# The first score pass of a 16-head attention, two heads at a time on the two 64-row halves of the TensorE array

## The chip, the cores and the metric

The kernel runs on one core of one Trainium2 chip. The metric is the device time of the whole program in microseconds; the median of several runs counts. The kernel is one program for all sixteen batch rows of a two-layer block, with everything written out ahead of time: each engine has one straight list of instructions, and the order in each list comes from timetables in the source.

## The reference, cut to what matters

The block has an attention and a feed-forward part in layer 0 (16 heads of 8 dimensions over 512 tokens, then eight experts of which each token uses one), and a windowed attention and a two-layer local transformer in layer 1. The change concerns the layer 0 attention alone:

```python
x_h = x.reshape(b, t, h, d).transpose(0, 2, 1, 3)      # 16 heads, d = 8, t = 512
xw  = jnp.einsum('bhtd,hde->bhte', x_h, w_att_val)
att = jnp.einsum('bhte,bhse->bhts', xw, x_h) / jnp.sqrt(d)
att = jax.nn.softmax(att, axis=-1)                     # then att @ values, projection
```

So each batch row needs, for each of 16 heads, a 512x512 matrix of scores, its row maxima, its exponentials and their product with the values.

## The kernel before

The scores are wanted at nearly float32 precision from bf16 products. Queries and keys are therefore split into three bf16 parts (`SPLIT = 3`), and all nine products of a part with a part are summed in one contraction: a "stack" of 3 x 3 x 8 = 72 rows (`STACK`) holds for each head the matching parts of the queries (`Qst_a`) and of the keys (`Kst_a`). The scores are computed twice. The first pass (L1436, and L1424 for group 0) contracts 72 rows with queries on the output partitions; VectorE takes the maximum of each 128x512 result (L1583, L1571). The maxima, in two bf16 parts, are turned by TensorE (`turned_parts`, L677), copied by ScalarE (L1518, L1535) and put by one DMA (`max_to_stack`, L1359) into rows 72 and 73 of `Qst_a`, beside rows of ones in `Kst_a`. The second pass (L1466) contracts these 74 rows with keys on the output partitions, so that the maxima come off in the product, and ScalarE takes the exponential (L1523). The products with the values are L1452, eight records for each key tile, on column strips of 32.

The heads are worked in four groups of four. A group has 16 first-pass and 16 second-pass products (4 heads x 4 tiles). The stacks lie in a ring of two. While group g is in its second pass, group g+1 is in its first pass: in `a_tensor` the two alternate, product by product. Group 0's first pass lies apart, in `head_tensor`, in the stage before.

The stacks are filled through DRAM. SyncE's queue issues 8 DMAs that spill the parts (`spill`, L1343 and L1345), and then for each group 6 DMAs that load the stack (`load_stack`, L1354 and L1355; each of 24 rows by 4 heads by 1 KB). Groups 0 and 1 are loaded once the spill is there, group 2 when the last second-pass product of group 0 is made, group 3 when the last of group 1 is made (`a_sync`). In SyncE's list the DMA for the maxima of group 1 stands behind the load of group 2, and that of group 2 behind the load of group 3. SyncE runs its list strictly in order.

Around this, in one stage of the loop (`rows`), five streams are woven: this attention for one batch row, the layer 1 windowed attention (`b`) and the `head` of following rows, and the local transformer (`f`, `feed`) of the rows before. `TIMES` gives each stream's slots a place, `merge` sorts them on each engine, and the result is the fixed order. The score products share six PSUM banks (`SEATS` gives each product its bank, `Banks.take` waits until the product before it in that bank has been read). The opening, which does row 0 among the gating and expert work, uses three banks in turn and its own tables (`OPEN`).

In TensorE's order of before, one stage counts 95 places where the next instruction uses another division of the array (full array, column strips of 32 or 64, row parts of 32 or 64, or both). Between the last second-pass product of group 1 and the first of group 3's first pass lie one transposition of 4, two L2023 groups of 16, L1452 x8, L677 x4, L2033 x8 and five transpositions of 4.

Of the kernel before, what the change touches and what calls it, by code (L numbers as in the profile page):

```python
# [23 lines left out]
P = 128  # L24
# [227 lines left out]
                  (-147.32851, -146.32851)),  # L252
            "head": ((0, 9.5, 12, 17, 29.6),
                  (-161.91197, -159.15848, -159.15847, -128.18067, -121.88243)),
            "f": ((0, 8.1, 14.2),
                  (-262.83466, -259.50354, -168.69272)),
            "a": ((34, 36, 56, 59, 83),
                  (-262.9151, -260.55741, -246.75033, -239.1571, -236.47977)),
            "finish": ((14.7, 15.7),
                  (-227.09831, -226.09831))},  # L260
        "gpsimd": {
            "gate": ((0, 1),
                  (-80.93999, -79.93999)),
            "b": ((0.5, 1.5),
                  (-35.02612, -34.02612)),
            "head": ((1, 2),
                  (5.75878, 6.75878)),
            "f": ((5, 6.5, 10.4, 11.9, 15.8, 17.3, 21.2, 22.7, 47, 70, 71.5, 75.4, 76.9, 80.8, 82.3, 86.2, 87.7),
                  (-152.95046, -106.77442, -105.48318, -102.87694, -87.68456, -81.66902, -67.27071, -43.44755, -39.3071, -23.9864, -17.3062, 7.99167, 10.6375, 17.73295,
                   17.73296, 17.73297, 19.90829)),  # L270
            "feed": ((6.8, 7.8),
                  (-153.62176, -152.62176))},
# [6 lines left out]
            "head": ((4.5, 6, 16, 16.7, 17.4, 18.1, 18.8, 19.5, 20.2, 20.9, 21.6, 22.3, 23, 23.7, 24.4, 25.1, 25.8, 26.5, 29),  # L279
# [108 lines left out]
    "b": "015310413113055204155111345013352422",  # L388
    "head": "05202254021041231030",
    "f": ("415401435215345124031214215041450140224254013451510305204325341205231045204354324130414230"  # L390
          "4532032410025041"),
    "feed": "033035420"}
B_AT = 5
LAYER = 65
# [2052 lines left out]
```

## Time and profile before

| | |
|---|---|
| median of 3 runs | 3223.6 us (3221.94 to 3223.61) |
| profiled execution | 3225.27 us, span 3223.5 us |
| TensorE busy | 2973.0 us, 92% of the span |
| VectorE, ScalarE busy | 2333.2 and 2309.6 us, 72% each |
| granted TensorE clock, mean | 0.964 |

The opening takes the first 366 us; after that the stages repeat, each some 176 us long. Busy shares say where time is occupied, not what ends a wait; the matmul records are pipelined and their ends are modelled, so for TensorE the distance from start to start is the price of an instruction, and a busy TensorE still has small gaps.

### The profile page before, as it was taken

To read this page: it belongs to the slowest core of one execution; us is meant where nothing else is said; L and a number is where in the kernel's file an instruction comes from. 1 tells how busy PE (TensorE), PEld (TensorE's weight loads), DVE (VectorE), ACT (ScalarE), POOL (GpSimd) and SP (SyncE) were. 2 spreads that over 40 slices of the span, in tenths; PEclk is the share of its full clock that TensorE was granted. 3 is DMA by queue.
4 is the path that set the end of the run, shared out by engine and by line. 5 is a ranking of instruction groups with operands and counts; after the bars stand their busy time and mean duration, and the time that the engine had idled before them with its cause. 6 is when DMAs were issued, how large, how long until landed. Compare 5 with 4: busy or idle time off the path is not lost.

```text
span 3223.5 us, 84708 instructions
## 1 busy us (share of the span) xinstructions
PE 2973.0 (92%) x34588; PEld 1863.0 (58%) x34588; DVE 2333.2 (72%) x4989; ACT 2309.6 (72%) x4768; POOL 1221.3 (38%) x778
## 2 busy tenths in 40 slices
PE   5799699999999999999999999999999999999976
PEld 5269446556565656565565656565555656565654
DVE  6732487878686878878786868788787868687744
ACT  4453277787777787877777777868777777778754
POOL 1124044433333443444433334334444333344344
PEclk9689799999999999999999999999999999999988
DMA  4437200101011111011010101111110101111000
GB/s 135 118 117 208 60 23 24 42 15 44 25 33 36 34 32 37 25 33 33 15 46 23 41 28 34 33 36 32 32 29 15 46 23 34 35 33 33 6 14 4
DMA packets 128575, 134.10 MB, mean 42 GB/s; under 512 B 18100, under 2 KB 111070, under 8 KB 128190
## 3 DMA queue, kind: packets, MB, share of 16 engines
q1 hardware_dynamic: 123648, 119.37, 13.5%
q0 software_dynamic: 4544, 9.32, 1.3%
q8 instruction: 278, 4.55, 0.6%
q14 instruction: 105, 0.86, 0.1%
HBM read 81.06 MB, written 30.28 MB: 35 GB/s over the span
## 4 chain that ended last, share of the span: by engine, by line
PE 53%; ACT 21%; DVE 8%; issue 3%; SPq 2%; DMA 2%; POOL 1%; ACTq 0%; POOLq 0%; DVEq 0%
PE bank L1452 6%; PE bank L1466 5%; ACT area L2109 5%; PE bank L2047 5%; PE bank L1436 4%; ACT prob_a L1523 4%; PE bank L2023 3%; PE bank L2091 3%; PE bank L2014 3%; PE bank L671 3%; PE bank L2033 3%; PE bank L1986 2%; PE bank L2004 2%; PE bank L1424 2%; PE bank L1744 2%
## 5 line engine op out<-in xcount | busy, mean ns | idle before, releaser
L1523 ACT ACTIVATE prob_a<-bank 128x512 f32<-128x512 f32 x1024 | 554.0, 606 | 137.0 <-PE bank L1466 134.0
L1583 DVE TENSOR_REDUCE nmax_a<-bank 128x1 f32<-128x512 f32 x768 | 497.8, 683 | 96.5 <-PE bank L1436 93.5
L1953 POOL TENSOR_TENSOR rn<-ss,minus_half 128x16 f32<-128x16 f32 x128 | 391.7, 3060 | 223.1 <-DVE ss L2221 222.8
L1976 POOL TENSOR_TENSOR rs_f<-rs_f,minus_half 128x4 f32<-128x4 f32 x32 | 32.5, 1017 | 1076.5 <-DVE rs_f L1311 1076.5
L1466 PE MATMUL bank<-Qst_a,Kst_a 74*128 74x512 bf16 x1024 | 375.5, 391 | 12.3 <-ACT prob_a L1523 8.6
L2109 ACT ACTIVATE area<-bank 128x512 f32<-128x512 f32 x640 | 350.5, 610 | 49.5 <-PE bank L2047 46.5
L1959 POOL TENSOR_TENSOR turn_f<-turn_f 128x512 f32<-128x512 f32 x256 | 332.1, 1317 | 127.1 <-DVE turn_f L2226 127.1
L2226 DVE TENSOR_TENSOR turn_f<-area,rotf 128x1024 f32<-128x1024 f32 x256 | 305.6, 1216 | 5.8 <-POOL area L1963 5.4
L1436 PE MATMUL bank<-Kst_a,Qst_a 72*128 72x512 bf16 x768 | 302.7, 394 | 5.0 <-DMA Kst_a<-dk_a 2.3
L1452 PE MATMUL bank<-prob_a,V_a 128*18 128x512 f32 x2048 | 278.0, 615 | 16.1 <-ACT prob_a L1523 13.2
L1963 POOL TENSOR_TENSOR area<-turn_f,rn 128x1024 f32<-128x1024 f32 x128 | 243.5, 1902 | 18.3
L2233 DVE TENSOR_REDUCE nmax_f<-bank 128x4 f32<-128x512 f32 x256 | 167.2, 685 | 70.8 <-PE bank L2004 70.7
L1436 PEld LDWEIGHTS bank<-Kst_a,Qst_a 72*128 72x128 bf16 x768 | 75.3, 98 | 219.9 <-ACT prob_a L1523 96.8
L2047 PE MATMUL bank<-wqkv_s,hT_f 128*128 128x512 f32 x384 | 178.8, 603 | 20.5 <-ACT hT_f L2109 20.5
L2047 PE MATMUL bank<-wqkv_s,hT 128*128 128x512 f32 x384 | 195.3, 605 | 0.0
L1466 PEld LDWEIGHTS bank<-Qst_a,Kst_a 74*128 74x128 bf16 x1024 | 96.4, 98 | 164.9 <-ACT prob_a L1523 64.0
L2091 PE MATMUL bank<-xnT_f,w_s 128*128 128x512 f32 (+1 forms) x384 | 183.2, 615 | 2.7 <-ACT xnT_f L2109 2.7
L1986 PE MATMUL bank<-ident,area 128*128 128x128 f32 x1024 | 155.3, 280 | 23.9 <-ACT kq_a L1512 12.9
L1571 DVE TENSOR_REDUCE nmax_a<-bank 128x1 f32<-128x512 f32 x256 | 159.8, 675 | 14.4 <-PE bank L1424 12.8
L1912 DVE TENSOR_REDUCE max_b<-bank 128x8 f32<-128x512 f32 x192 | 130.7, 681 | 53.7 <-PE bank L1734 53.4
L2217 DVE TENSOR_REDUCE ss_tiny<-area 128x16 f32<-128x1024 f32 x128 | 154.1, 1204 | 15.6 <-ACT area L2109 15.6
L1808 ACT ACTIVATE oT_a<-bank 128x512 f32<-128x512 f32 x96 | 58.2, 606 | 132.7 <-PE bank L1744 132.6
(307 smaller groups left out, 6766.0 us busy)
## 6 DMA issues: line engine op xcount, KB each, us to landing
Qst_a<-dq_a SPq DMA_DIRECT2D x192, 96.0 KB
Kst_a<-dk_a SPq DMA_DIRECT2D x192, 96.0 KB
area<-in_W SPq DMA_DIRECT2D x25, 512.0 KB, 4.7
dq_a<-prob_a SPq DMA_DIRECT2D x80, 128.0 KB
V_f<-in_W SPq DMA_DIRECT2D x14, 512.0 KB, 4.9
dk_a<-prob_a SPq DMA_DIRECT2D x48, 128.0 KB
ys_d<-otok_f SPq DMA_DIRECT2D x39, 128.0 KB, 3.8
x_a<-in_x_in SPq DMA_DIRECT2D x16, 256.0 KB, 2.8
```

Source lines behind the costliest of these rows:

```text
L1436: nc.tensor.matmul(bk.take(pe, f)[:], Qst_a[0:STACK, g % RING, j, t * P:(t + 1) * P], Kst_a[0:STACK, g % RING, j, :], start=True, stop=Tru ...
L1452: last = nc.tensor.matmul(acc_a[32 * j:32 * j + 2 * (D0 + 1), :], V_a[:, k, 4 * g + j, :], prob_a[:, (4 * k + j) % PR_A, :], start=(g % 2 ...
L1466: nc.tensor.matmul(bk.take(pe, s)[:], Kst_a[0:ROWS, g % RING, j, k * P:(k + 1) * P], Qst_a[:, g % RING, j, :], start=True, stop=True).then ...
L1523: nc.scalar.activation(dst, bk.full(act, product)[rows, :], func, **kw).then_inc(a_emptied["act"], 1)
L1583: nc.vector.tensor_reduce(out=nmax_a[:, g, t, j:j + 1], in_=bk.full(dve, f)[:], op=ALU.max, axis=AX.X, negate=True).then_inc(emptied, 1)
L1953: nc.gpsimd.tensor_tensor(rn[:, t % 2], ss[:, t % 2], minus_half[:], ALU.pow).then_inc(f_root, 1)
L1959: last = nc.gpsimd.tensor_tensor(cos[:, :, :, lo:lo + 32], cos[:, :, :, lo:lo + 32], sin[:, :, :, hi:hi + 32], ALU.add)
L1963: nc.gpsimd.tensor_tensor(qk_raw[:, t % 2].rearrange("p a (h d) -> p a h d", d=FD), turned[:, :, 0].rearrange("p a (h d) -> p a h d", d=FD ...
L2047: nc.tensor.matmul(fk.take(pe, (product, l, t))[:], (hT if l == 0 else hT_f)[:, t * P:(t + 1) * P], wqkv_s[:, l, n * INNER:(n + 1) * INNER ...
L2091: nc.tensor.matmul(fk.take(pe, (product, l, c))[0:n, :], w1_s[:, l, col:col + n], xnT_f[:], start=True, stop=True).then_inc(f_filled, 1)
L2109: ins = nc.scalar.activation(dst, fk.full(act, product)[rows, cols], func, **kw)
L2226: last = nc.vector.tensor_tensor(turned[:, a].rearrange("p c (h d) -> p c h d", d=FD), raw[:, a].rearrange("p (h d) -> p h d", d=FD).unsqu ...
```

## The change

Heads of a group are taken in pairs, an even and an odd one. Even heads keep their stack in rows 0 to 71 with the maxima in rows 72 and 73. Odd heads have theirs in the upper half: the first 64 stack rows in array rows 64 to 127, the last 8 in rows 0 to 7, the maxima in rows 32 and 33 beside ones, and zeros in the other rows of 0 to 63, written once at the start. The first pass contracts 64 rows only (the product of the last parts is left out of it, and the parts are spilled in another order so that this is the smallest one), the even head on rows 0 to 63 and the odd head on rows 64 to 127, one right after the other into two banks. Both banks are taken before the first of the two is issued. The second pass of odd heads contracts all 128 rows. A group's stack is loaded by 14 DMAs in place of 6 (even and odd heads apart, and the odd heads' last part in two pieces), and its maxima by two DMAs in place of one. The first-pass products of a group stand in the order head 0, head 1 for each query tile, then heads 2 and 3, and a pair has one slot, before two second-pass products.

All tables of `TIMES` and `SEATS` are new; `OPEN` and `STEP` are as before. The numbers in the tables are places in an order, and the streams' order is what they amount to. On TensorE one stage now crosses 136 times between divisions of the array, and 32 pairs stand where 64 products stood. Group 0's eight pairs come after the last windowed scores of stream `b`, where before the first two of its products stood ahead of them. Between the last second-pass product of group 0 and group 2's first pair stand two transpositions of 4 and two L2047 products more than before; between the last of group 1 and group 3's first pair the same pieces as before, in another order (transposition, L2023 x16, L1452 x8, L677 x4, L2023 x16, L2033 x8, five transpositions). SyncE's order around the loads is unchanged: load of group 2, maxima of group 1, load of group 3, maxima of group 2, maxima of group 3.

```diff
@@ TIMES (all streams of all engines are new; one of them) @@
-            "head": ((4.5, 6, 16, 16.7, 17.4, 18.1, 18.8, 19.5, 20.2, 20.9, 21.6, 22.3, 23, 23.7, 24.4, 25.1, 25.8, 26.5, 29),
...
+            "head": ((4.5, 6, 16, 17.4, 18.8, 20.2, 21.6, 23, 24.4, 25.8, 29),
+                  (12.75675, 14.24365, 45.14976, 45.14977, 50.14609, 50.47676, 50.59673, 55.58908, 55.58909, 58.57354, 64.32902)),
...
-        Kst_a, Qst_a = sb("Kst_a", [P, RING, 4, T], BF16), sb("Qst_a", [ROWS, RING, 4, T], BF16)
+        Kst_a, Qst_a = sb("Kst_a", [P, RING, 4, T], BF16), sb("Qst_a", [P, RING, 4, T], BF16)
...
+            for tile in (Kst_a, Qst_a):
+                nc.vector.memset(tile[0:64, :, 1::2, :], 0.0)
...
+            nc.vector.memset(Kst_a[32:34, :, 1::2, :], 1.0)
...
-        first = [[("first", g, j, t) for j in range(4) for t in range(NT)] for g in range(G)]
+        first = [[("first", g, 2 * i + odd, t) for i in range(2) for t in range(NT) for odd in range(2)] for g in range(G)]
...
-                sp.dma_start(dq[:, c], parts_q[:, c % SPLIT, :]).then_inc(s, 16)
+                sp.dma_start(dq[:, c], parts_q[:, (c + 1) % SPLIT, :]).then_inc(s, 16)
...
-        SPILLED, STACKED = (3 * SPLIT - 1) * 16, 2 * SPLIT * 16
-
-        def load_stack(sp, dq, dk, h, n, Qst, Kst, s):
+        SPILLED, STACKED = (3 * SPLIT - 1) * 16, 14 * 16
+
+        def load_stack(sp, dq, dk, h, Qst, Kst, s):
 
             rows = SPLIT * D0
-            q_rows, k_rows = (d[h:h + n].rearrange("h c d t -> (c d) h t") for d in (dq, dk))
-            for i in range(SPLIT):
-                sp.dma_start(Qst[rows * i:rows * i + rows], q_rows[D0 * i:D0 * i + rows]).then_inc(s, 16)
-                sp.dma_start(Kst[rows * i:rows * i + rows], k_rows).then_inc(s, 16)
+            for odd in range(2):
+                q_rows, k_rows = (d[h + odd:h + 4:2].rearrange("h c d t -> (c d) h t") for d in (dq, dk))
+                for i in range(SPLIT):
+                    for lo, hi, at in (((0, 16, 112), (16, 24, 0)) if odd and i == SPLIT - 1 else ((0, rows, 64 * odd + rows * i),)):
+                        sp.dma_start(Qst[at:at + hi - lo, odd::2], q_rows[D0 * i + lo:D0 * i + hi]).then_inc(s, 16)
+                        sp.dma_start(Kst[at:at + hi - lo, odd::2], k_rows[lo:hi]).then_inc(s, 16)
...
-            sp.dma_start(Qst[STACK:ROWS, :, :], mT).then_inc(landed, 16)
+            for odd, at in enumerate((STACK, 32)):
+                sp.dma_start(Qst[at:at + 2, odd::2, :], mT[4 * odd:4 * odd + 4, :]).then_inc(landed, 16)
...
+        def first_pair(r, pe, bk, g, n):
+            if n == 0:
+                pe.wait_ge(*nth(r, a_stack[g], STACKED))
+            pair = [(bk.take(pe, f), f) for f in first[g][n:n + 2]]
+            for ps, (_, _, j, t) in pair:
+                rows = slice(64 * (j % 2), 64 * (j % 2) + 64)
+                nc.tensor.matmul(ps[:], Qst_a[rows, g % RING, j, t * P:(t + 1) * P], Kst_a[rows, g % RING, j, :],
+                                 start=True, stop=True).then_inc(a_filled, 1)
+
...
             for g in range(G):
                 for n in range(16):
-                    yield A_GROUP[g] + 1.2 * n
-                    if g + 1 < G:
-                        first_pass(g + 1, n)
+                    if g + 1 < G and n % 2 == 0:
+                        yield A_GROUP[g] + 1.2 * n
+                        first_pair(r, pe, bk, g + 1, n)
                     yield A_GROUP[g] + 1.2 * n + 0.4
                     if n == 0:
-                        pe.wait_ge(*nth(r, a_mrow[g], 16))
+                        pe.wait_ge(*nth(r, a_mrow[g], 32))
                     _, _, k, j = s = second[g][n]
-                    nc.tensor.matmul(bk.take(pe, s)[:], Kst_a[0:ROWS, g % RING, j, k * P:(k + 1) * P], Qst_a[:, g % RING, j, :],
+                    nc.tensor.matmul(bk.take(pe, s)[:], Kst_a[0:(P if j % 2 else ROWS), g % RING, j, k * P:(k + 1) * P],
+                                     Qst_a[0:(P if j % 2 else ROWS), g % RING, j, :],
                                      start=True, stop=True).then_inc(a_filled, 1)
```

## Rows read from the trace of the kernel before

**Rows 1.** The page: busy time of the engines; granted TensorE clock in 40 slices, in tenths.
```profile
PE 2973.0 (92%) x34588; PEld 1863.0 (58%) x34588; DVE 2333.2 (72%) x4989; ACT 2309.6 (72%) x4768; POOL 1221.3 (38%) x778
...
PEclk9689799999999999999999999999999999999988
```

**Rows 2.** Windows: one stage; length, busy of PE, PEld, DVE, ACT, POOL, clock, DMA.
```profile
1062.04:1238.35 176.32, 167.89 (x2078) 102.58 (x2075) 139.05 (x289) 137.52 (x288) 70.76 (x44) 1.00 0.12 32
```

**Rows 3.** The chain that ended last by engine (page), and one of the waits.
```profile
PE 53%; ACT 21%; DVE 8%; issue 3%; SPq 2%; DMA 2%; POOL 1%; ACTq 0%; POOLq 0%; DVEq 0%
...
ACT prob_a L1523 <- PE bank L1466: 134.0, 194, 2.7
```

**Rows 4.** Groups by line and shape, PE: count, busy us, mean ns, idle before.
```profile
L1466 PE MATMUL bank<-Qst_a,Kst_a 74*128 74x512 bf16 x1024 | 375.5, 391 | 12.3 <-ACT prob_a L1523 8.6 <-DVE nmax_a L1583 2.9 <-DMA Qst_a<-Kst_a 0.5
L1436 PE MATMUL bank<-Kst_a,Qst_a 72*128 72x512 bf16 x768 | 302.7, 394 | 5.0 <-DMA Kst_a<-dk_a 2.3 <-ACT prob_a L1523 2.1 <-DVE nmax_a L1583 0.6
...
L1424 PE MATMUL bank<-Kst_a,Qst_a 72*128 72x512 bf16 x256 | 85.4, 410 | 22.5 <-DMA Kst_a<-dk_a 20.4 <-DVE nmax_a L1571 1.6 <-ACT og_a L1808 0.3
```

**Rows 5.** The chain in order of time, in group 2's first pass: start, length.
```profile
1343.02 0.22 PE bank L1466
1343.24 0.98 PE bank L1452 x8
1344.22 0.32 PE bank L1436
```

**Rows 6.** Timeline of PE where two row parts of the array work together.
```profile
1239.32 1.05 PE L1417 MATMUL bank<-wv_s,kq_a 128*128 128x128 f32 x8
1240.30 0.39 PE L1702 MATMUL bank<-lat_q,lat_of 32*128 32x512 bf16 x2
1240.53 1.02 PE L1707 MATMUL bank<-spare_b,prob_a 32*128 32x256 f32 x8
```

**Rows 7.** Timeline of SyncE's queue: load of group 3 (first and last of 6), maxima of group 2.
```profile
1345.23 0.30 SPq L1354 DMA_DIRECT2D Qst_a<-dq_a  x1
...
1347.24 0.38 SPq L1355 DMA_DIRECT2D Kst_a<-dk_a  x1
1348.73 0.63 SPq L1359 DMA_DIRECT2D Qst_a<-Kst_a  x1
```

**Rows 8.** Windows of 1 us over that load (last columns: DMA share, GB/s).
```profile
1348.23:1349.23 1.00, 1.00 (x11) 1.00 (x11) 0.00 (x0) 0.98 (x2) 0.00 (x0) 1.00 0.82 167
...
1350.23:1351.23 1.00, 1.00 (x12) 0.99 (x11) 0.69 (x4) 0.83 (x3) 0.00 (x0) 1.00 0.00 0
```

**Rows 9.** Timeline of PE: group 1's last second pass, then groups 3 and 2.
```profile
1344.82 0.38 PE L1466 MATMUL bank<-Qst_a,Kst_a 74*128 74x512 bf16 x1
...
1351.18 0.38 PE L1436 MATMUL bank<-Kst_a,Qst_a 72*128 72x512 bf16 x1
1351.40 0.38 PE L1466 MATMUL bank<-Qst_a,Kst_a 74*128 74x512 bf16 x1
```

**Rows 10.** Timeline of the opening: a DMA of maxima and the product that waits.
```profile
98.79 0.77 SPq L1359 DMA_DIRECT2D Qst_a<-Kst_a  x1
...
100.94 0.61 PE L1466 MATMUL bank<-Qst_a,Kst_a 74*128 74x512 bf16 x1 [0.51 <-DMA Qst_a<-Kst_a]
```

**Rows 11.** The chain in order of time: the last DMA of a load of group 0.
```profile
2866.91 4.48 DMA Kst_a<-dk_a
```

**Rows 12.** Timeline of VectorE in group 0's first pass: eight maxima, the split.
```profile
1283.46 4.86 DVE L1571 TENSOR_REDUCE nmax_a<-bank 128x1 f32<-128x512 f32 x8
...
1293.45 0.17 DVE L1335 TENSOR_REDUCE mparts_a<-nmax_a 128x16 bf16<-128x16 f32 x1
```

**Rows 13.** Windows of 5 us: VectorE (fourth figure) before and during group 0's pass.
```profile
1268.00:1273.00 5.00, 4.78 (x159) 3.67 (x158) 3.93 (x10) 4.35 (x13) 0.00 (x0) 1.00 0.51 141
...
1283.00:1288.00 5.00, 5.00 (x82) 3.99 (x84) 4.96 (x11) 2.31 (x4) 0.00 (x0) 1.00 0.02 5
```

**Rows 14.** Timeline of VectorE at the start, behind the memsets.
```profile
13.57 1.64 DVE L1077 BATCH_NORM_STATS2 spare_b<-V_s 128x6 f32<-128x128 f32 x8 [6.31 <-DMA V_s<-in_x_in]
```

More of the change, by code:

```diff
@@ L676, in turned_parts @@
             for t in range(NT):
-                last = nc.tensor.matmul(dst[MT, t * P:(t + 1) * P], parts[:, t].rearrange("p a j -> p (a j)"), ident_bf[:],
+                last = nc.tensor.matmul(dst[MT, t * P:(t + 1) * P], parts[:, t].rearrange("p o a j -> p (o a j)"), ident_bf[:],
                                         start=True, stop=True)
@@ L1265, in mixer_kernel @@
             for n in range(16):
-                if g + 1 < G:
-                    plan_a.append((A_GROUP[g] + 1.2 * n, first[g + 1][n], ["dve"]))
+                if g + 1 < G and n % 2 == 0:
+                    plan_a += [(A_GROUP[g] + 1.2 * n, f, ["dve"]) for f in first[g + 1][n:n + 2]]
                 plan_a.append((A_GROUP[g] + 1.2 * n + 0.4, second[g][n], ["act"]))
@@ L1418, in head_tensor @@
             last.then_inc(a_filled, 1)
-            for n, f in enumerate(first[0]):
-                _, _, j, t = f
+            for n in range(0, 16, 2):
                 yield 16 + 0.7 * n
-                if n == 0:
-                    pe.wait_ge(*nth(r, a_stack[0], STACKED))
-                nc.tensor.matmul(bk.take(pe, f)[:], Qst_a[0:STACK, 0, j, t * P:(t + 1) * P],
-                                 Kst_a[0:STACK, 0, j, :], start=True, stop=True).then_inc(a_filled, 1)
+                first_pair(r, pe, bk, 0, n)
             yield 29
@@ L1430, in a_tensor @@
         def a_tensor(r, pe, bk, hk):
-            def first_pass(g, n):
-                _, _, j, t = f = first[g][n]
-                if n == 0:
-                    pe.wait_ge(*nth(r, a_stack[g], STACKED))
-                nc.tensor.matmul(bk.take(pe, f)[:], Qst_a[0:STACK, g % RING, j, t * P:(t + 1) * P],
-                                 Kst_a[0:STACK, g % RING, j, :], start=True, stop=True).then_inc(a_filled, 1)
             def max_rows(g):
@@ L1570, in head_vector @@
                 yield 16 + 0.7 * n
-                nc.vector.tensor_reduce(out=nmax_a[:, 0, t, j:j + 1], in_=bk.full(dve, f)[:], op=ALU.max, axis=AX.X,
+                nc.vector.tensor_reduce(out=nmax_a[:, 0, t, top_at(j):top_at(j) + 1], in_=bk.full(dve, f)[:], op=ALU.max, axis=AX.X,
                                         negate=True).then_inc(emptied, 1)
@@ L1574, in head_vector @@
             dve.wait_ge(*bk.brought(first[0][-1], "dve"))
-            yield from split_max(28.1, link, nmax_a[:, 0], [mparts_a[:, 0, :, p, :] for p in range(2)], h_mparts)
+            yield from split_max(28.1, link, nmax_a[:, 0], [mparts_a[:, 0, :, :, p, :] for p in range(2)], h_mparts)
         def a_vector(r, dve, bk, link, after_finish=False):
@@ L1582, in first_pass @@
                 _, _, j, t = f = first[g][n]
-                nc.vector.tensor_reduce(out=nmax_a[:, g, t, j:j + 1], in_=bk.full(dve, f)[:], op=ALU.max, axis=AX.X,
+                nc.vector.tensor_reduce(out=nmax_a[:, g, t, top_at(j):top_at(j) + 1], in_=bk.full(dve, f)[:], op=ALU.max, axis=AX.X,
                                         negate=True).then_inc(emptied, 1)
@@ L1587, in max_parts @@
                 dve.wait_ge(*bk.brought(first[g][-1], "dve"))
-                yield from split_max(A_GROUP[g - 1] + 19.6, link, nmax_a[:, g], [mparts_a[:, g, :, p, :] for p in range(2)], a_mparts)
+                yield from split_max(A_GROUP[g - 1] + 19.6, link, nmax_a[:, g], [mparts_a[:, g, :, :, p, :] for p in range(2)], a_mparts)
             for g in range(G):
```

76 lines of the change are left out of this document (39 added, 37 removed), and 125 rows, old and new, of the table TIMES.

## The prediction

> **What bounds the kernel now.** I read the page first: TensorE is busy 92% of the span, VectorE and ScalarE 72% each, and after the opening's slices its granted clock is at full (9 or more tenths) until the end [rows 1]. Then the windows of one stage: of 176.3 us TensorE is busy 167.9, VectorE 139.1, ScalarE 137.5, at a granted clock of 1.00 [rows 2]. Then the chain that ended last: TensorE carries 53% of it, ScalarE 21%, VectorE 8%, and the largest waits between engines are those of ScalarE's exponentials for their scores [rows 3]. So TensorE's issue order sets the pace, with the two others near enough to take over where the order gets denser. The stage repeats from 366 us to about 3000 us, and fifteen batch rows pass through it; the sixteenth lies in the opening. A microsecond per stage is 15 us, or 0.5%.
>
> The groups by line [rows 4] show what is touched: 768 + 256 first-pass products and 1024 second-pass ones. Their means (391 to 410 ns) are latencies; the price is the distance from start to start, 0.22 us each in the chain [rows 5].
>
> **What the pairs save.** Two products on different row parts of the array overlap: the two 32-row products of L1702 start together at 1240.30 and the next instruction starts at 1240.53, so 512 bf16 columns through two row parts cost 0.23 us in place of 0.44 [rows 6]. That is with 32-row parts and not 64, the nearest row there is. 64 products become 32 pairs, 32 x 0.21 = 6.7 us a stage. If the halves did not overlap, nothing of this would be saved; the row speaks against that.
>
> **What they cost TensorE.** Each change of the array's division has a price. In the chain a first-pass product that follows a plain one takes 0.22, one that follows the column strips of L1452 takes 0.32 [rows 5]; going into row parts, eight records of L1417 at 0.11 are 0.88 and the next start is 0.98 behind the first [rows 6]. So about 0.095 a crossing. The old order has 95 crossings a stage and the new one 136, counted in the two timetables: 41 x 0.095 = 3.9 us. A pair inside full-array work pays 0.19 for a gain of 0.21; it is the eight pairs of group 0, which lie partly together, and those that stand beside L1452 or another strip, that earn. Net 6.7 - 3.9 = 2.8 us. The 128-row second pass of odd heads costs nothing: a full-array product of as many columns costs the same whatever the rows in it are (L1436 with 72 rows and L1466 with 74, 0.22 both), and I know no dearer row.
>
> The Trainium skill says the same in TensorEngine Tiling (Array Packing), Key Properties: changing the tiling mode drains the array. It gives no price. With the 0.095 of the row the rule eats more than half of the gain; read as free, the sum would be 15 x 3.9 = 58 us lower.
>
> **What the loads cost.** A load is 14 DMAs on one queue in place of 6. The six of group 3 start 0.40 us apart (five steps from 1345.23 to 1347.24), one takes 0.30 to 0.38 [rows 7]. I take 0.40 for the smaller ones too, since no row shows a DMA's issue getting cheaper with fewer rows; the lower bound is 0.34 (0.30 and 0.04 between), the upper 0.67, the pitch of the DMA for the maxima, which has only eight runs [rows 7]. Landing of the last one: a small one lets its waiter go 2.15 us after it started (98.79 to 100.94) [rows 10]; the last of six takes 4.48 [rows 11], but there six large ones are backed up, and the transfers run at 167 GB/s until they are through [rows 8]. Fourteen halves at one in 0.40 us ask for about 120 GB/s (48 KB each) and don't back up, so I take 2.1. Load to landing: 13 x 0.40 + 2.1 = 7.3 us, where six took between 5 and 6.
>
> *Group 3.* The load starts at 1345.23, when group 1's last second-pass product is through, and group 3's first product stands at 1351.18: 5.95 us [rows 9]. The new order has the same pieces there and two more crossings, 6.15 us. So TensorE waits 7.3 - 6.15 = 1.15 us. Then comes what is queued behind the loads: the maxima of group 2. Before, the queue was free at 1347.6 and their DMA went out at 1348.73 [rows 7]. Now the queue is free 5.6 us after the load's start, the second of two DMAs starts 0.67 later, at 6.3, and lets go at 8.4. The first second-pass product of group 2 would stand 0.32 behind the pair, at 7.6; it waits 0.8 more. Together 2.0 us a stage, all on TensorE, with nothing to cover it since its list is in order. With 0.34 a DMA: 4.4 + 2.1 = 6.5 and 7.6, together 0.9. With 0.67: 10.8 and 12.2, together 5.7.
>
> *The other groups.* Between its release and its first product group 2's load had about 7 us of pieces (the pieces of both orders reckoned at the chain's prices, here and below) and now gets two transpositions and two 0.86 us products more, almost 10: covered. Group 0's pairs stand 4.5 us later in the order, its load lands 1 us later: covered, and the wait that L1424 shows now, 20.4 us over the run of which most in the opening [rows 4], goes where it was in the stages, 0.3 us each. Group 1's load has 15 us to spare. The two DMAs of maxima cost 0.67 more before each second pass; the spaces there grew by 0.2 to 0.8 and had 0.8 to spare: nothing.
>
> **VectorE in group 0's pass.** Eight maxima take 4.86 us, 0.61 each [rows 12]. From TensorE's first pair to L677 the new order needs 11.1 us, the old 16.6. VectorE has 16 x 0.61 = 9.7 in that stretch, 1.2 of other work laid between, and the split, 0.9 with its neighbour: 11.8. It becomes the bound by 0.7, of which 0.2 was already lost there. Before the pass it has room that it can't use (3.93 of 5 us), in the pass none (4.96 of 5) [rows 13]. I count +0.5, from 0 (if it runs ahead) to 3.0 (if other work slides in). The pairs take two banks at once; where VectorE is late by one reduction, TensorE waits for both. With six banks I count this within that range.
>
> **Start and opening.** The memsets lie ahead of a 6.31 us wait of VectorE [rows 14]: nothing. In the opening the three loads with little room cost up to 2 us each and the pairs save some of it at half clock; three banks make pairs stiffer. I take +2, from -5 to +8.
>
> **Sum.** A stage: -2.8 - 0.3 + 2.0 + 0.5 = -0.6 us. Fifteen: -9. With +2 for the opening, -7 on the profiled 3225.27 us, which lies 1.7 above the median: 3218 by the profile, 3216.6 against the median. Predicted: 3217 us.
>
> **Rivals.** (1) *The loads don't hold TensorE.* If small DMAs issue in 0.34 and the wait at group 3 lets ScalarE and VectorE catch up, so that later waits (for `prob_a`, 134 us over the run in ScalarE's favour [rows 3]) shrink by as much: -2.8 to -3.1 a stage, 15 x -2.9 + 2 = -42, 3182 us. For it: at 1350 VectorE has little to do [rows 8] and could bank time; against it: TensorE is busy nearly all of that stretch, and a wait in an in-order list is rarely given back.
>
> (2) *The queue is the bound: slower.* Place: group 3's first pair and group 2's first second-pass product. Price: 5.7 us a stage at 0.67 a DMA. Stage: -3.1 + 5.7 + 0.5 = +3.1; fifteen and +4 in the opening give +50, 3274 us. It decides from 0.44 us a DMA on: there the wait is 2.6 and the stage is no faster. For it: the issue price has not followed size in any row; half way, at 0.53, it is 3245.
>
> (3) *Nothing comes out.* The results must still be read: 16 maxima a group at 0.61 us and 16 exponentials besides. Where a pair and two second-pass products stand close (0.23 + 0.19 + 0.44 = 0.86 us), VectorE needs 1.2. A shorter TensorE then waits at the banks for what it saved; stage within 0.3 of before, 3224 us. The Trainium skill has this as PSUM Bottleneck, in TensorEngine Tiling (Array Packing): tiling speeds TensorE up, not the reading of PSUM. For it: VectorE at 4.96 of 5 [rows 13]; against it: 37 us of slack a stage [rows 2].
>
> **How the numbers follow.** Forecast 0.36, rival 1 0.20, rival 2 0.24, rival 3 0.20. Its own range for the forecast is 3200 to 3232. The range that holds 8 in 10 goes from 3178 (most of rival 1) to 3262 (rival 2 up to a DMA price of about 0.6). About 0.2%, 6.5 us, is what a measurement can tell. Faster by more: 0.21 of the forecast's 0.36, 0.20, 0.02 of rival 3: 0.43. Within: 0.11 and 0.13: 0.24. Slower: 0.04, 0.24 and 0.05: 0.33.
>
> **What would show it.** After: pairs 3 to 5 ns apart with the next start 0.23 or 0.32 us on; stages of 175 to 176 us; an idle of about 1.2 us before group 3's first pair with a stack DMA as its releaser, and about 0.8 before group 2's second pass with the DMA of the maxima; L677 of group 0 waiting for VectorE. The prediction is wrong in its core if the issue pitch of the 14 DMAs isn't near 0.40, if the halves don't overlap, or if the waits at the banks of the score products grow by more than a microsecond a stage.

## The result, and the profile after

The changed kernel takes 3269.35 us (median of 3257.69, 3269.35 and 3271.68) against 3223.6: 1.0134 times before, interval 1.0096 to 1.0172. It is slower, by 46 us, where 3217 was forecast; the time also lies above the range. In a later job, copies of both kernels side by side gave 1.0138 (1.0111 to 1.0164). One caution goes with every ratio below: the kernel before has two levels, 3223 to 3229 us in some jobs and 3281 to 3291 in others, and the changed kernel takes 3268 beside either. Each run names its "before"; what the higher level is comes at the end.

The page after answers to [rows 1, 3]. TensorE's busy time reads 2943 us for 2973, but 172 matmul records of L1469 are missing from this trace; in the copy of the changed kernel, whose records are complete, it is 2967. So TensorE is busy for about as long as before, in a longer span. Its share of the chain fell from 53 to 48%, ScalarE's rose from 21 to 26%. Then the groups of the two passes, which answer to [rows 4].

```profile
PE 2943.1 (90%) x34416; PEld 1821.9 (56%) x34588; DVE 2348.5 (72%) x4992; ACT 2321.1 (71%) x4768; POOL 1243.0 (38%) x778
...
PEclk9699799999999999999999999999999999999988
...
PE 48%; ACT 26%; DVE 6%; issue 4%; SPq 3%; DMA 1%; POOL 1%; POOLq 0%; ACTq 0%; DVEq 0%
...
L1469 PE MATMUL bank<-Qst_a,Kst_a 74*128 74x512 bf16 (+1 forms) x852 | 292.0, 395 | 23.9 <-DMA Qst_a<-Kst_a 8.7
L1455 PE MATMUL bank<-prob_a,V_a 128*18 128x512 f32 x2048 | 277.7, 615 | 26.1 <-ACT prob_a L1527 18.9
L1419 PE MATMUL bank<-Kst_a,Qst_a 64*128 64x512 bf16 x1024 | 203.4, 399 | 54.3 <-DMA Kst_a<-dk_a 19.7
```

One stage of after, as a window (columns as in [rows 2]): as long as a stage of before plus 1.8 us. (Ten PE records are missing from it.)

```profile
1082.49:1260.57 178.08, 166.39 (x2068) 99.92 (x2075) 139.97 (x289) 138.38 (x288) 72.23 (x44) 1.00 0.11 31
```

The place that the prediction names, group 3's load and group 2's maxima, in the timeline of SyncE's queue and of PE (answers to [rows 7, 9]). Fourteen DMAs, 0.41 us apart (one takes 1.17), then the two of the maxima; the first pair 7.7 us after the load's start. This is one of the stages with a slow DMA; most have none, and their first pair stands at 7.17 us (below).

```profile
1544.28 0.30 SPq L1355 DMA_DIRECT2D Qst_a<-dq_a  x1
1544.62 0.37 SPq L1356 DMA_DIRECT2D Kst_a<-dk_a  x1
1545.04 0.37 SPq L1355 DMA_DIRECT2D Qst_a<-dq_a  x1
...
1548.35 1.17 SPq L1355 DMA_DIRECT2D Qst_a<-dq_a  x1
...
1550.39 0.29 SPq L1356 DMA_DIRECT2D Kst_a<-dk_a  x1
1550.72 1.28 SPq L1364 DMA_DIRECT2D Qst_a<-Kst_a  x2
```

```profile
1552.01 0.39 PE L1419 MATMUL bank<-Kst_a,Qst_a 64*128 64x512 bf16 x2 [0.62 <-DMA Kst_a<-dk_a]
1553.16 0.39 PE L1469 MATMUL bank<-Qst_a,Kst_a 74*128 74x512 bf16 x1 [0.76 <-DVE nmax_a L1587]
```

The pairs themselves, in the chain in order of time: both products in the time of one, and 0.32 us to the next start.

```profile
1543.39 0.32 PE bank L1419 x2
1543.71 0.55 PE bank L1469
```

**Where the time went.** I cut each of the 14 inner stages at the starts of four kinds of TensorE instructions: the stage's first product (xw), the turning of a group's maxima (mT0 to mT3) and a group's first second-pass product (s0 to s3). Mean lengths in us; "before" and "changed" are the two copies that ran on one chip (b_copy, a_copy), "order" and "loads" are two experiments that follow:

| stretch | before | changed | order alone | loads alone |
|---|---|---|---|---|
| xw to mT0 (group 0's first pass in it) | 56.84 | 56.61 | 56.60 | 59.37 |
| mT0 to s0 | 4.23 | 4.93 | 4.93 | 4.24 |
| s0 to mT1 (group 1's first pass) | 24.10 | 23.64 | 23.91 | 24.09 |
| mT1 to s1 | 4.69 | 4.83 | 4.85 | 5.77 |
| s1 to mT2 (group 2's first pass) | 20.36 | 20.64 | 20.97 | 20.48 |
| mT2 to s2 (maxima, behind group 3's load) | 3.73 | 5.72 | 4.55 | 6.10 |
| s2 to mT3 (group 3's first pass) | 15.22 | 15.57 | 15.95 | 17.00 |
| mT3 to the next xw | 46.84 | 46.73 | 46.73 | 46.84 |
| stage | 176.01 | 178.67 | 178.49 | 183.90 |
| opening, to the first xw | 363.6 | 370.7 | 370.6 | 372.7 |

TensorE's own work, estimated with each instruction at the distance from start to start that its kind has when nothing waits, plus 0.093 us a crossing, is 165.0 us a stage before and 162.4 changed; the rest, waiting and low clock, is 11.0 and 16.3. So by this estimate the stage lost 2.6 us of work, near the forecast, and gained 5.3 us of waits. (The crossing's price goes into it, so it is no independent test of that price.) Of the stretches, mT2 to s2 grew most, by 2.0 us, of which the order alone brings 0.8.

### The profile page after: what moved, and what is told of

Its sections match the earlier page's. It is cut to its first block, busy times and chain, and to the rows that moved or that the text cites. A ratio compares the mean times of both kernels' runs of the same rounds, so it can differ in the third digit from the quotient of the medians.

```text
span 3269.9 us, 85578 instructions
## 1 busy us (share of the span) xinstructions
PE 2943.1 (90%) x34416; PEld 1821.9 (56%) x34588; DVE 2348.5 (72%) x4992; ACT 2321.1 (71%) x4768; POOL 1243.0 (38%) x778
## 4 chain that ended last, share of the span: by engine, by line
PE 48%; ACT 26%; DVE 6%; issue 4%; SPq 3%; DMA 1%; POOL 1%; POOLq 0%; ACTq 0%; DVEq 0%
ACT prob_a L1527 7%; ACT area L2113 6%; PE bank L1455 5%; PE bank L2095 5%; PE bank L1469 4%; PE bank L2051 4%; PE bank L667 3%; PE bank L2027 3%; PE bank L1419 3%; DVE nmax_a L1575 3%; PE bank L2101 2%; PE bank L2008 2%; PE bank L2018 2%; PE bank L1738 2%; PE bank L1748 2%
## 5 line engine op out<-in xcount | busy, mean ns | idle before, releaser
L1587 DVE TENSOR_REDUCE nmax_a<-bank 128x1 f32<-128x512 f32 x768 | 493.6, 682 | 111.5 <-PE bank L1419 109.7
L2113 ACT ACTIVATE area<-bank 128x512 f32<-128x512 f32 x640 | 349.3, 618 | 43.7 <-PE bank L2051 37.3
L1469 PE MATMUL bank<-Qst_a,Kst_a 74*128 74x512 bf16 (+1 forms) x852 | 292.0, 395 | 23.9 <-DMA Qst_a<-Kst_a 8.7
L1419 PE MATMUL bank<-Kst_a,Qst_a 64*128 64x512 bf16 x1024 | 203.4, 399 | 54.3 <-DMA Kst_a<-dk_a 19.7
L2051 PE MATMUL bank<-wqkv_s,hT_f 128*128 128x512 f32 x384 | 185.8, 615 | 28.1 <-ACT hT_f L2113 20.5
L1419 PEld LDWEIGHTS bank<-Kst_a,Qst_a 64*128 64x128 bf16 x1024 | 50.4, 93 | 275.0 <-DVE nmax_a L1587 89.5
L1469 PEld LDWEIGHTS bank<-Qst_a,Kst_a 74*128 74x128 bf16 (+1 forms) x1024 | 80.0, 97 | 196.3 <-ACT prob_a L1527 76.5
L2162 ACT ACTIVATE area<-bank,nmax_f 128x128 f32<-128x128 f32 x512 | 144.9, 380 | 30.3 <-DVE nmax_f L2237 29.0
L1575 DVE TENSOR_REDUCE nmax_a<-bank 128x1 f32<-128x512 f32 x256 | 157.1, 677 | 1.9 <-PE bank L1419 1.9
```

The costliest lines, as they stand in the source:

```text
L1419: nc.tensor.matmul(ps[:], Qst_a[rows, g % RING, j, t * P:(t + 1) * P], Kst_a[rows, g % RING, j, :], start=True, stop=True).then_inc(a_fill ...
L1469: nc.tensor.matmul(bk.take(pe, s)[:], Kst_a[0:(P if j % 2 else ROWS), g % RING, j, k * P:(k + 1) * P], Qst_a[0:(P if j % 2 else ROWS), g % ...
L1575: nc.vector.tensor_reduce(out=nmax_a[:, 0, t, top_at(j):top_at(j) + 1], in_=bk.full(dve, f)[:], op=ALU.max, axis=AX.X, negate=True).then_i ...
L1587: nc.vector.tensor_reduce(out=nmax_a[:, g, t, top_at(j):top_at(j) + 1], in_=bk.full(dve, f)[:], op=ALU.max, axis=AX.X, negate=True).then_i ...
L2051: nc.tensor.matmul(fk.take(pe, (product, l, t))[:], (hT if l == 0 else hT_f)[:, t * P:(t + 1) * P], wqkv_s[:, l, n * INNER:(n + 1) * INNER ...
L2113: ins = nc.scalar.activation(dst, fk.full(act, product)[rows, cols], func, **kw)
```

## The experiments

Five jobs, each kernel beside runs of the kernel before on the same chip.

**e1: a pair's banks one by one.**

```diff
-            pair = [(bk.take(pe, f), f) for f in first[g][n:n + 2]]
-            for ps, (_, _, j, t) in pair:
+            for f in first[g][n:n + 2]:
+                ps, (_, _, j, t) = bk.take(pe, f), f
```

> The changed kernel, but the second product of a pair takes its bank only after the first is issued, so the first never waits for the second's bank. Compared per stage with the changed kernel's 178.9 us. Theory A (the products' readers, VectorE above all, set the pace, so that TensorE's shorter work returns as waits): no change, 178.5 to 179.2, total 3262 to 3275. Theory B (the pair takes two banks at once, and this coupling makes the waits that ate the saving): 1.5 to 4 us a stage less, total 3210 to 3245. Theory C (the redrawn order is worse by itself): no change.

0.992 (0.989 to 0.995) of a before at 3282; stage 178.4. Against the changed kernel's 178.7 that is 0.3 at most. The two times come from different jobs, but the changed kernel has nearly the same time in all of its jobs (3268 to 3269). Taking both banks at once is not the cause.

**e2 and e8: the order alone,** once in the first job and again in the third.

```diff
 (the kernel before with)
+TIMES, SEATS of the changed kernel; first[g] in its order
+                    if g + 1 < G and n % 2 == 0:
+                        first_pass(g + 1, n)
+                        first_pass(g + 1, n + 1)
```

> The kernel before with nothing but the new timetables and seats: 72-row products, two in a row where the pair stood, six loads, one DMA for the maxima. Theory A: TensorE gets its 0.2 us a product back as work, the stage comes to the 176 us of before or a little over (176 to 178), total 3220 to 3255, and the wait ahead of group 3's first pass is gone. Theory B: the same as A. Theory C: the order carries the loss; 178.5 us a stage or more, total above 3262, even without the longer loads.

0.998 (0.996 to 1.000) of a before at 3282, stage 179.3. By its ratio no loss, by its stage 3 us of loss: not to be read without a profile of before on the same level.

> The redrawn order alone once more (72-row products one behind the other, 6 DMAs a load, one DMA of maxima), because in the first job the kernel before itself took 3282 us and not 3223. In the second job the changed kernel showed, against the kernel before on the same chip: TensorE's own work -2.6 us a stage (2.8 predicted), the stretch from group 2's maxima to its second pass +2.2 (2.0 predicted), and 4 us of new short waits in the first passes that nothing in the forecast covers. Theory C (the redrawn order and its banks bring the short waits): stage 179 to 179.5 as in the first job, ratio 1.015 to 1.02 to before where before takes 3223. Theory R (the pairs bring them, since VectorE and ScalarE must read what comes sooner): this kernel has the stage of before, 176 to 176.5, ratio 1.000 to 1.004.

1.0117 (1.0095 to 1.0140) of a before at 3229, stage 178.5: on theory C's side, a little below its numbers. The order alone, timetables and bank table together, costs 2.5 us a stage and 7 in the opening, nearly all that the changed kernel loses. Which of the two costs it is open. It has before's instructions and one crossing fewer (94 for 95), so the 2.5 us are waits. Most of them are too short to show as idle time of PE, whose ends are modelled; the weight loads (PEld) show some of what they stood for. For the first-pass products, stretch 540 to 2980 us, the order alone and then before (who waits for whom, us in total, times, longest):

```profile
PEld bank L1433 <- DVE nmax_a L1581: 62.7, 81, 1.0
...
PEld bank L1433 <- ACT prob_a L1521: 38.5, 54, 0.9
```

```profile
PEld bank L1436 <- ACT prob_a L1523: 79.1, 140, 1.0
...
PEld bank L1436 <- DVE nmax_a L1583: 6.3, 28, 0.3
```

The reader is to see the change of hands: in before the bank of a first product was held by a maximum in 28 places and briefly, in the new order it is in 81. The total grew less, from 85 to 101 us, since the waits for ScalarE halved; in the changed kernel's copy it is 116. Most of such a wait doesn't reach the products. By the distance from start to start (an estimate), what does comes to 1.0 us a stage at L1433 (under 0.2 at L1436), 1.9 for 1.2 at the product with the values, 2.6 for 1.9 at L2045 and 1.6 for 0.8 at L2012. Other places lost waits: by a like estimate group 0's first products have 0.1 for 0.8, L1984 0.4 for 1.2 and L1464 1.0 for 1.5. So the order's loss is the balance of many small waits and not one wait at one place.

**e3: maxima over 256 of 512 columns** (half of the scores stay out of the maxima).

```diff
-  in_=bk.full(dve, f)[:], op=ALU.max
+  in_=bk.full(dve, f)[:, 0:T // 2], op=ALU.max
```

> The changed kernel, with the maxima of the first pass taken over 256 of the 512 columns, so that 64 reductions a stage cost about 0.34 instead of 0.61 us on VectorE (17 us of VectorE a stage less). It leaves half of the scores out of the maxima. Theory A: the saving of the pairs comes through: 2 to 4 us a stage less outside the wait for group 3's load, 175 to 177 us, total 3205 to 3240. Theory B: part of it too, since banks come free sooner, 1 to 2 us. Theory C, or ScalarE as the pace: under 1 us less, total above 3255.

0.990 (0.988 to 0.992) of a before at 3282; stage 177.9, opening 358.3 for 370.7. VectorE alone holds 0.7 us a stage, and 12 us in the opening: in the stages too little for theory A, in the total too much for C.

**e4: group 3 loads only the even heads' 6 DMAs** (the odd heads keep group 1's stack).

```diff
-            for odd in range(2):
+            for odd in range(1 if h == 12 else 2):
...
-                pe.wait_ge(*nth(r, a_stack[g], STACKED))
+                pe.wait_ge(*nth(r, a_stack[g], LOADED[g]))
```

> The changed kernel, with 6 of the 14 DMAs for group 3 (the even heads' alone; the odd heads of group 3 compute with the stacks of group 1). Every theory takes the wait between the turning of group 2's maxima and group 2's second pass to fall from 5.6 to about 3.6 us. If waits in an in-order list are not given back, the stage falls by the whole 2.0 us, total 3232 to 3245. If later waits for the readers grow in its place (A at its strongest), by 0 to 1 us, total 3255 to 3270.

0.989 (0.986 to 0.991) of a before at 3282; stage 177.2, mT2 to s2 4.66, where 3.6 had been expected. Group 3's longer load is worth 1.5 us a stage, 1.1 of it in mT2 to s2. Here nothing waits for the load, and the first pair still stands 7.18 us behind the load's start (timelines of SyncE's queue and of PE):

```profile
1173.92 0.30 SPq L1357 DMA_DIRECT2D Qst_a<-dq_a  x1
1181.10 0.39 PE L1421 MATMUL bank<-Kst_a,Qst_a 64*128 64x512 bf16 x2
1181.42 0.39 PE L1471 MATMUL bank<-Qst_a,Kst_a 74*128 74x512 bf16 x1
```

The copy of the changed kernel has the same 7.17 in most stages, and waits only at the maxima:

```profile
1186.19 0.30 SPq L1355 DMA_DIRECT2D Qst_a<-dq_a  x1
1193.36 0.39 PE L1419 MATMUL bank<-Kst_a,Qst_a 64*128 64x512 bf16 x2
1194.24 0.61 PE L1469 MATMUL bank<-Qst_a,Kst_a 74*128 74x512 bf16 x2 [0.48 <-DMA Qst_a<-Kst_a]
```

**b_copy and a_copy: both kernels unchanged on one chip.**

> The kernel before, unchanged, for a profile on the chip of this job. In the job of the first four experiments it took 3282 us (median of 13), where the runs beside the prediction took 3223.6, and there is no profile of it at that level. If the difference is one of the chip or of the execution, its stages are some 3 to 4 us longer here than the 176.13 of the first profile and the opening about the same; the zones in which this shows tell what else varies: I expect them in the stretch from xw to group 0's maxima, whose length varies most from stage to stage. If it comes out at 3224 again, the level of 3282 belongs to that one chip.

> The changed kernel, unchanged, beside a profile of the kernel before on the same chip. Theory C (the redrawn order itself loses some 3 us a stage): 1.005 to 1.015 times before, stages 2 to 3 us longer than in b_copy. Theory D (the loss of 1.3% was mostly between the executions of two jobs, the change itself is worth -1 to +0.5 us a stage): 0.990 to 1.000 times before, as the change with banks taken one by one was (0.992) in the last job; stage 178 to 179 us against the same or more in b_copy. In both the stretch from group 2's turned maxima to its second pass is 2 us longer than before's, which both theories put down to the load of group 3.

3223.2 and 3268.4, ratio 1.0138: theory C's numbers, and the first profile's stages again (176.01, 178.67).

**e6: the two late DMAs of a load on a semaphore of their own, behind group 2's maxima, and the banks as in e1.**

```diff
-        STACKED = 14 * 16
+        STACKED = 12 * 16
...
+                if g == 2:
+                    a_rest_load(sp, 3)
```

> The changed kernel with two edits: the pair's banks are taken one by one, and the two DMAs of each load that only the second pass needs (rows 0 to 7 of the odd heads) have a semaphore of their own; for group 3 they are issued behind the maxima of group 2, for the other groups right behind the load. First pairs wait for 12 DMAs in place of 14 (2 x 0.41 = 0.8 us sooner), and group 2's maxima go out 0.8 us sooner. If the load of group 3 costs what was predicted (2.0 us a stage, 2.1 measured), the stretch from group 2's turned maxima to its second pass shortens by about 0.8 of its 5.6 us, and the kernel is some 12 us faster than a_copy, with the banks up to 7 more. If the wait is taken over by another (readers behind), the stretch shortens but the stage does not.

3256.8 for a_copy's 3268.4 in the same job, 1.0105 (1.0076 to 1.0134) of before; mT2 to s2 4.96 for 5.72. As expected: 0.76 us where 0.8 was reckoned, 12 us in all; the stage fell by 0.5.

**e7: no overlap,** both products of a pair on rows 0 to 63 (the odd heads' maxima come from other rows).

```diff
-                rows = slice(64 * (j % 2), 64 * (j % 2) + 64)
+                rows = slice(0, 64)
```

> The changed kernel in which both products of a pair use rows 0 to 63, so that they cannot lie beside each other; the odd heads' maxima are taken from other rows and the output is not the reference's, everything else issues as before. TensorE gets 32 x 0.21 = 6.7 us of work a stage more. If TensorE's time sets the pace in the first passes (my forecast), the stage is 6 to 6.7 us longer, 90 to 100 us in all (ratio to a_copy 1.03). If the readers of the scores set it there (rival 3), the pairs' time hides under VectorE's maxima: the stage is longer by 2 us or less (under 35 us, ratio under 1.01).

3332.0, +63.6 us, 1.019 times a_copy: neither theory. A stage is 4.1 us longer for a nominal 6.7 of work. The overlap is real and about 60% of it reaches the clock; waits take up the rest.

**e5: the pairs in the order of before,** and **e10**, the same with e6's edits.

```diff
-TIMES, SEATS of the changed kernel
+TIMES of the kernel before (a pair where its first product stood), its SEATS with changes
```

> The changed kernel with the timetable and the banks of the kernel before: a pair stands where its first product stood; six of the 290 banks of a stage are moved because two products would wait for each other. 141 crossings a stage in place of 95: TensorE 6.7 - 46 x 0.095 = 2.3 us shorter; loads and maxima DMAs as in the change, +2.2 at group 3. Theory C: the new short waits are gone, stage about 176.0, ratio 0.998 to 1.003, 10 to 13 per mille under the changed kernel. Theory R: the short waits come with the pairs, stage 178 to 180, ratio 1.010 to 1.02.

> The pairs in the old order (as the run beside it) with banks taken one by one and the two late DMAs of a load on a semaphore of their own, behind group 2's maxima. Theory C: 0.6 to 0.8 us a stage less than that run, 10 us, so 0.994 to 1.000 times before: the best the change can give without a new timetable. Theory R: no better than 1.008.

1.071 (1.068 to 1.073) and 1.062 (1.059 to 1.065) of a before at 3229; stages 190.5 and 188.9. Far outside both theories. Six banks were to be moved; in the kernel that ran 36 of the 290 entries of the bank table differ from before's, 22 of them outside this attention. In e5's trace, against the same stretch as above:

```profile
PE bank L1422 <- DMA Kst_a<-dk_a: 37.5, 20, 4.2
PE bank L1993 <- DVE nmax_a L1590: 27.0, 13, 2.1
```

The longer loads find no room here, as e9 shows by itself. L1993 belongs to another stream and waits for a bank that a maximum holds; whether the pairs that were pulled forward cause this or the moved banks is open. So these two runs don't tell how the change would do in the old order with the old banks.

**e9: the loads alone,** the kernel before with each load cut into 14 DMAs and the maxima into two.

```diff
+                    for lo, hi in (((0, 16), (16, 24)) if odd and i == SPLIT - 1 else ((0, rows),)):
+                        sp.dma_start(Qst[rows * i + lo:rows * i + hi, odd::2], ...).then_inc(s, 16)
```

> The kernel before with each load of a stack cut into 14 DMAs of the change's sizes and the maxima's DMA into two; products, rows and order are its own. By the prediction only group 3's load and group 2's maxima have no cover: +1.2 us before group 3's first product and +0.8 before group 2's second pass, 2.0 to 2.2 us a stage, 30 to 33 us in all, ratio 1.009 to 1.011. If the wait is taken out of other waits (rival 1), under 0.5 us a stage, ratio under 1.003.

1.034 (1.032 to 1.036) of a before at 3229, 3340 us: 7.9 us a stage where 2.0 to 2.2 were expected. Its waits:

```profile
PE bank L1427 <- DMA Kst_a<-dk_a: 24.6, 9, 4.1
PE bank L1439 <- DMA Kst_a<-dk_a: 22.8, 19, 2.8
...
PE bank L1469 <- DMA Qst_a<-Kst_a: 14.3, 24, 0.7
```

They sum to 62 us over the 13.3 stages of that stretch, 4.6 a stage (before has 7 us of such waits, 0.5 a stage); group 0's load (L1427) and group 1's maxima behind group 2's load are late here too. Of the rest, 1.8 us lie in s2 to mT3, behind the late load: the granted clock is 0.96 over these stages where before has 0.99. In the windows of s2 to mT3 of two stages of this kernel the same 144 products stand (last columns: clock, DMA share, GB/s):

```profile
1035.83:1054.03 18.20, 18.20 (x143) 7.74 (x144) 13.10 (x26) 11.84 (x26) 0.00 (x0) 0.81 0.00 1
1405.84:1420.98 15.14, 15.14 (x144) 6.62 (x144) 13.12 (x26) 11.44 (x26) 0.00 (x0) 1.00 0.01 2
```

Ahead of the first one TensorE had idled twice in 4 us (timeline of PE):

```profile
1034.73 0.39 PE L1439 MATMUL bank<-Kst_a,Qst_a 72*128 72x512 bf16 x1 [1.89 <-DMA Kst_a<-dk_a]
1035.83 0.39 PE L1469 MATMUL bank<-Qst_a,Kst_a 74*128 74x512 bf16 x1 [0.71 <-DMA Qst_a<-Kst_a]
```

10 of 14 stages of e9 have s2 to mT3 at 16.7 us or more, 4 have 15.1. The changed kernel has 15.2 in 12 of them and 17.8 in two; there the windows of half a microsecond (a_copy) show the clock fall to 0.50, which is 1.2 GHz, behind idles of 1.54 and 1.05 us:

```profile
650.50:651.00 0.50, 0.00 (x0) 0.00 (x0) 0.14 (x1) 0.28 (x1) 0.00 (x0) 1.00 0.27 53
...
652.50:653.00 0.50, 0.00 (x0) 0.00 (x0) 0.50 (x2) 0.00 (x0) 0.00 (x0) 1.00 0.03 8
653.00:653.50 0.50, 0.36 (x2) 0.11 (x2) 0.41 (x1) 0.00 (x0) 0.00 (x0) 0.81 0.42 160
653.50:654.00 0.50, 0.50 (x4) 0.03 (x2) 0.00 (x0) 0.29 (x1) 0.00 (x0) 0.50 0.95 361
```

**e11, e12, e13: both readers halved** (maxima and exponentials over 256 of 512 columns) in the changed kernel, in before and in the order alone; the other half of the exponentials is left out.

```diff
+ in_=bk.full(dve, f)[:, 0:T // 2] (maxima)
+ prob_a[:, n % PR_A, 0:T // 2] <- bk.full(act, second[g][n])[:, 0:T // 2] (exponentials)
```

> The changed kernel, VectorE's maxima and ScalarE's exponentials of the first attention over 256 of the 512 columns (the output is not the reference's). 64 maxima and 64 exponentials a stage are shorter by 0.25 to 0.3 us each, about 17 us for either engine. Theory R (the readers' speed makes the short waits): the stage falls from 178.7 to 174 or less, the first-pass stretches lose their 4 us of waits, and the difference to the kernel before with the same edit is under 0.5 us a stage above the 2.2 of the load. Theory C (the lists stand badly to each other, whatever the speed): it falls by about as much as in the kernel before, and a difference of 2 to 3 us a stage is left.

> The kernel before with the same edit of both readers (output not the reference's). TensorE's own work is 165 us a stage of 176: what is left above it is 11. If the readers' speed is behind a part of these waits in the kernel before too, the stage falls to 173 to 175; the waits for other engines' chains (hT_f, xnT_b, kq_a) stay, since they don't pass through these readers.

> The redrawn order alone (72-row products, loads of 6) with the same edit of both readers (output not the reference's). Theory R: the order's 2.5 us a stage over the kernel before shrink to under 1. Theory C: 2 us or more of them stay.

0.982 (0.979 to 0.985), 0.990 (0.987 to 0.993) and 0.973 (0.970 to 0.976) of a before at 3291; stages 176.6, 179.3 and 175.7. The control, e12, is only half a control: it carries, in s1 to mT2, the 4 us of the higher level (next runs). Leaving that stretch out, the order alone stands 1.1 us above before with halved readers and 1.9 with whole ones. That lies between the two theories. By stretches it is clearer. In the order alone the three first passes become shorter by 3.3 us together (23.91 to 22.52, 20.97 to 20.08, 15.95 to 14.91); in before the two that can be compared shorten by 0.56 and 0.22. Against before, the order's s0 to mT1 and s2 to mT3 go from -0.19 and +0.73 to -1.02 and -0.09, 1.65 us less. So what the order loses in those two passes hangs on the readers of the score products, VectorE's maxima and ScalarE's exponentials together, and shorter reading removes it. What is left of its loss is mT0 to s0 and mT2 to s2 (1.5 us, unchanged by the halving) and xw to mT0, which is now 0.9 us longer than before's and with whole readers was 0.2 shorter; why, is open. The loads' wait is untouched in e11 (mT2 to s2 6.30), and its stage fell by 2.1, not by the 4.7 of theory R.

**b_again and a_again: both kernels once more.**

> The kernel before, unchanged. If the job is of the kind in which it takes 3280 to 3290 us: ScalarE shows one wait of about 3.5 us a stage whose releaser is no engine, in the stretch from group 1's second pass to group 2's maxima, the stretch is 24 to 25 us and not 20.6, the stage about 180. If the job is of the other kind: stage 176.0 as before, and the wait stays unexplained.

> The changed kernel, unchanged, stage 178.7 in either kind of job, no such wait; ratio to before 1.013 where before takes 3223, about 0.994 where it takes 3285.

3281.4 and 3268.1: this job was of the other kind, and the ratio of the change is 0.996 (0.995 to 0.998). Before's stage is 179.9, with s1 to mT2 24.5 for 20.4; the changed kernel's is 178.1. In ScalarE's timeline of before, one exponential a stage starts late with no engine as its releaser ("remote"); b_copy, at the lower level, has the same instructions without it:

```profile
1355.19 1.08 ACT L1523 ACTIVATE prob_a<-bank 128x512 f32<-128x512 f32 x2 [2.85 <-remote]
```

```profile
1333.20 1.09 ACT L1523 ACTIVATE prob_a<-bank 128x512 f32<-128x512 f32 x2 [0.15 <-PE bank L1466]
```

It occurs 13 times in the 13 to 14 stages of that stretch, at the same instruction, 37.3 us in all; TensorE waits 32.8 us for it (L1436), and in s1 to mT2 its clock falls to 0.93 in most stages. e12, before with halved readers, has it 14 times; no trace of a kernel with the redrawn order has it from stage to stage. What ScalarE waits for is open. Its 3.9 us a stage, 14 times, are 55 of the 58 us by which before is at 3281 and not at 3223, and so why the same change is 1.4% slower beside one before and 0.4% faster beside the other.

## Why the prediction was wrong

- **The step that failed: the order itself, which has no term in the sum.** The prediction moved TensorE's pieces at their own prices and, group 0's pass apart, set the new places of everything else at nothing. e8 shows that the move alone, with no pair and no longer load, costs 2.5 us a stage and 7 us of the opening. I had the orders of all engines in the timetables and reckoned only TensorE's through. That part of it hangs on the readers of the score products is shown for the passes s0 to mT1 and s2 to mT3 (e13 against e12); the balance by places, and the shares of the timetables and of the bank table, are open.
- **What the pairs save, and the crossings:** right, as far as the estimate goes. 6.7 - 3.9 = 2.8 us a stage forecast, 2.6 estimated in TensorE's own work. The pair takes 0.32 to the next instruction of another division [the chain above] and 0.23 to the next pair. Overlap on 64-row halves is as good as on 32. e7 shows that 4.1 of the 6.7 us reach the time.
- **Issue and landing of the 14 DMAs:** the sum was right, its terms only in part. 0.41 us apart for 0.40; load to landing 7.3 us for 7.3 (mean for group 3). But the last DMA lands 1.6 us after its start and not 2.1, so most loads are there at 6.9, and in six of 14 stages one DMA's issue takes a microsecond, which makes up the mean.
- **Group 3's wait:** 1.1 us, where 2.0 was forecast. The pieces before the first pair take 7.17 us and not 6.15 (e4; the order alone has 6.78), so in 8 of 14 stages the load is there first and the pair waits for nothing; over all stages it waits 0.4 and not 1.15. The maxima behind the load wait 0.7 for a forecast 0.8. With the low clock that follows in two stages, e4 prices the load at 1.5.
- **The other groups are covered:** right in the new order for groups 1 and 2. e9 shows what this was worth: in the old order they are not, and the load costs 7.9 us a stage. That is what the redrawn order bought.
- **L1424's 0.3 us goes:** no. In xw to mT0 the first products are 0.65 us late a stage, for 0.79 before.
- **VectorE in group 0's pass, +0.5:** about right in size; e3 prices all of VectorE's holding at 0.7 us a stage. That a pair takes two banks at once was counted as within the range, and e1 bears it out (0.3 at most).
- **The sign of being wrong:** the waits at the banks of the score products did grow, as weight loads see them by 31 us from 540 to 2980 us at the first-pass products, 2.3 us a stage. Most of such a wait doesn't reach the products' starts.
- **Opening:** +2 forecast, +5 (+7 in the copies), again the order's.

The sum by what the runs show: order +2.5 a stage. Pairs and loads on top of it +0.2: mT2 to s2 is 1.2 longer than in the order alone, the three first passes s0 to mT1, s1 to mT2 and s2 to mT3 are 1.0 shorter together, and xw to mT0, where eight pairs stand, is as long. Together 2.7 a stage; 14 stages 37 us, opening 5 to 7, the rest in the last stages.

Of the rivals, the third named a mechanism that is part of it (TensorE waits at the banks) and priced it at nothing lost; none has the order alone as a cost. Rival 2's 3274 lies near the measured time by luck: its place was right, but the DMAs issue at 0.41 us and not at 0.67, and the load costs 1.5 us a stage and not 5.7. The Trainium skill's PSUM Bottleneck, in TensorEngine Tiling (Array Packing), says that tiling does not speed up the reading of PSUM. No run here shows this apart: e8 and e13, which bear on the readers, have no pairs, and in e7 60% of a pair's gain reaches the time all the same. None of the kernels with the whole work beats before at its lower level; e6 with 1.0105 is the nearest, and what is left in it is mostly the order.

## What to carry to other kernels

A redrawn order has a price of its own, and it has to be measured alone, with the old work in it, before anything is said of the edit that it was redrawn for; reckon each engine's list through, not only the busiest one's. A wait of TensorE may cost twice its length, since the granted clock can fall behind it: in e9 waits of 1.89 and 0.71 us were followed by 3.1 us of longer work. And profile the kernel before in the same job: its level can move by 1.8% through a single wait that the changed kernel doesn't have.

## What the hardware showed that I had not expected

- Two idles of TensorE, of 1.89 and 0.71 us within 4 us (e9) or of 1.54 and 1.05 us (a_copy), were followed by a granted clock of 0.50 for some microseconds. In e9 the same work then took 18.2 us, with a mean clock of 0.81, for 15.1; 10 of its 14 stages have it to some extent. In other stages similar waits left the clock at 1.00: in a_copy a stretch mT2 to s2 of 6.4 us had 15.2 behind it, one of 6.6 had 17.8.
- The same exponential of ScalarE waits 2.85 us a stage for nothing that the profile names, in some jobs and not in others. It isn't the chip alone: one chip gave before 3229 us in one job and 3291 in the next.
- A DMA's issue takes 0.41 us from start to start whether it carries 96 or 48 KB, and one in the middle of fourteen took 1.17. Six of the 16 loads of group 3 have such a slow one (1.07 to 1.79 us).
